# Four attention and feed-forward layers on one core: when the queue of SyncE issues the context, shared-weight and row loads of the first and fourth attention

## The reference

```
x = x + L0_attention(layernorm(x), ctx)   # 16 heads of 16, masked
x = x + L0_ffn(layernorm(x))              # 8 experts, top 1, and a shared part
x = x + L1_attention(layernorm(x), ctx)   # one head of 256
x = x + L1_ffn(layernorm(x))              # 8 experts, top 2, and a shared part
x = x + L2_attention(layernorm(x), ctx)   # 16 heads of 64
x = x + L2_ffn(layernorm(x))              # 8 experts, top 2
x = x + L3_attention(layernorm(x), ctx)   # 16 heads of 16, masked
x = x + L3_ffn(layernorm(x))              # one dense part, then a last layer norm
```

## Time and profile before

| what | value |
|---|---|
| median of 3 runs | 2320.24 us (2318.2 to 2321.33) |
| profiled execution, its own time | 2323.39 us |
| its span, first to last instruction | 2321.6 us |
| TensorE busy (matmul) | 2169.4 us, 93% |
| VectorE, ScalarE, GpSimd busy | 1285.7, 1074.0, 448.3 us |
| mean granted TensorE clock | 0.969 of full speed |
| DMA, share of 16 engines from 100 to 200 us | 0.72, at 182 GB/s |
| DMA, share of 16 engines from 2000 to 2100 us | 0.73, at 184 GB/s |

### The profile page before, as it was taken

One profiled execution on the slowest core, in us unless ns is written; L12 is line 12 of the kernel. 1 busy time (PEld: TensorE's weight loads), 2 busy tenths in 40 slices (PEclk: granted clock), 3 DMA queues, 4 the chain that ended last, 5 costly groups with the idle time before them and its releaser, 6 DMA issues.

```text
span 2321.6 us, 46633 instructions
## 1 busy us (share of the span) xinstructions
PE 2169.4 (93%) x16038; PEld 1759.9 (76%) x16038; DVE 1285.7 (55%) x3563; ACT 1074.0 (46%) x2929; POOL 448.3 (19%) x478
## 2 busy tenths in 40 slices
PE   7999989999988899999999999999959979988998
PEld 6888877777666667678888788888747758877888
DVE  6877873222244522556556556555542238778766
ACT  5878872222223122244444444444402237877863
POOL 3112201111153345100000000000014421121150
PEclk9999999999999799999999999999969989999999
DMA  8677746222265322110000000001232257767701
GB/s 211 184 193 181 183 116 276 79 86 91 71 178 166 128 66 68 41 46 8 19 27 16 12 14 13 12 8 48 95 113 62 64 143 185 188 175 178 179 19 33
DMA packets 154867, 230.65 MB, mean 99 GB/s; under 512 B 66608, under 2 KB 127488, under 8 KB 152336
## 3 DMA queue, kind: packets, MB, share of 16 engines
q1 hardware_dynamic: 142160, 196.07, 30.4%
q0 software_dynamic: 10656, 29.37, 4.1%
q10 hardware_dynamic: 1824, 2.23, 0.4%
HBM read 176.36 MB, written 51.25 MB: 98 GB/s over the span
## 4 chain that ended last, share of the span: by engine, by line
PE 77%; DVE 7%; DMA 5%; issue 4%; SPq 3%; ACT 2%; POOL 1%; ACTq 0%; DVEq 0%; POOLq 0%
PE bank L2012 9%; PE bank L1157 8%; PE bank L2045 6%; PE bank L1188 6%; PE bank L1043 6%; PE bank L1039 6%; PE bank L2077 5%; PE bank L1083 4%; PE bank L1142 4%; PE bank L1028 3%; PE bank L1135 3%; PE bank L2062 3%; SPq L1523 2%; DMA query_halves<-arena 2%; PE bank L2398 2%
## 5 line engine op out<-in xcount | busy, mean ns | idle before, releaser
L1157 PE MATMUL bank<-ident,arena 112*125 112x112 f32 x2352 | 376.0, 278 | 2.2 <-DVE arena L1395 0.3
L1157 PEld LDWEIGHTS bank<-ident,arena 112*125 112x125 f32 x2352 | 342.8, 191 | 32.2 <-ACT arena L1428 5.8
L1428 ACT ACTIVATE arena<-arena,mx 112x375 f32<-112x375 f32 x512 | 309.3, 605 | 108.6 <-DVE mx L1374 104.5
L1374 DVE CUSTOM_DVE_ANT_0 arena<-bank,maskf 112x375 f32<-112x375 f32 x512 | 272.8, 541 | 101.3 <-PE bank L1135 96.8
L1428 ACT ACTIVATE arena<-bank,mx 112x375 f32<-112x375 f32 x272 | 154.8, 573 | 183.0 <-DVE mx L1386 155.4
L2012 PE MATMUL bank<-arena 128*128 x532 | 231.7, 558 | 2.1 <-ACT arena L2138 2.1
L1135 PE MATMUL bank<-kS,qS 128*112 128x376 f32 x512 | 204.9, 401 | 28.6 <-DMA qS<-query_halves 13.9
L1395 DVE COPY arena<-bank 125x336 f32<-125x336 f32 x448 | 214.1, 501 | 17.3 <-PE bank L1157 17.3
L1188 PE MATMUL bank<-arena 125*32 125x112 f32 (+1 forms) x4608 | 202.6, 265 | 3.1 <-DVE arena L1395 2.9
L1188 PEld LDWEIGHTS bank<-arena 125*32 125x32 f32 (+1 forms) x4608 | 144.3, 118 | 49.8 <-issue 32.5
L1435 ACT ACTIVATE arena<-bank 125x336 f32<-125x336 f32 x336 | 148.3, 442 | 45.4 <-PE bank L1157 44.4
(11 more groups left out here) (266 smaller groups left out, 3699.2 us busy)
## 6 DMA issues: line engine op xcount, KB each, us to landing
kS<-key_halves SPq DMA_DIRECT2D x256, 188.0 KB, 3.9
key_halves<-arena SPq DMA_DIRECT2D x64, 376.0 KB, 4.9
arena<-in_ctxT SPq DMA_DIRECT2D x62, 376.0 KB, 4.9
arena<-in_f_out SPq DMA_DIRECT2D x21, 768.0 KB, 4.5
qS<-query_halves SPq DMA_DIRECT2D x252, 56.0 KB, 2.2
arena<-in_f_up SPq DMA_DIRECT2D x4, 2816.0 KB, 20.0
arena<-results SPq DMA_DIRECT2D x38, 224.0 KB, 5.6
query_halves<-arena SPq DMA_DIRECT2D x32, 224.0 KB, 5.3
```

The source lines that it names most:

```text
L1157: m = pe.transpose(bank[2 + g % 2][0:KT, k * S:(k + 1) * S], pr[:, g % t.NR, k * KT:(k + 1) * KT], ident[0:S, 0:S])
L1374: dve.tensor_tensor_reduce(sm[:, g % 2, :], bank[g % 2][0:S, 0:SK], maskf[:, :], -t.a["scale"], 3e38, ALU.add, ALU.min, mx[:, g % t.NR:g % ...
L1428: act.activation(pr[:, g % t.NR, :], src, ACT.Exp, bias=mx[:, g % t.NR:g % t.NR + 1], scale=-1.0, accum_out=row_sum(t, b)[:, h:h + 1]).the ...
```

## The change

The loads that followed `batch(b)` become a function `loads(b)`. For b = 0, 1 and 2 it is called where the loads stood. `loads(3)` to `loads(14)` are called inside the next group, behind its spill of the queries and its spill of the first keys and ahead of its stackings. Nothing else moves; `loads(15)`, which would issue nothing, is not called.

```
                 spill_queries()
                 spill_keys(0)
+                if b > LOADS_LATE:
+                    loads(b - 1)
                 if b >= 2:
                     sp.wait_ge(t.scores, t.h0 + (b - 1) * t.H)
                 stack_queries()
...
-            for b in range(B):
-                batch(b)
+            LOADS_LATE = 3
+
+            def loads(b):
                 if t.L == 0 and b + 2 < B // 2:
                     rows_of_x(sp, b + 2)
...
+            for b in range(B):
+                batch(b)
+                if b < LOADS_LATE:
+                    loads(b)
```

## The result

| | before | after |
|---|---|---|
| median | 2320.78 us (2318.2 to 2325.83, 4 runs) | 2304.88 us (2301.49 to 2305.7, 4 runs) |
| ratio | | 0.9918 [0.9901, 0.9934] |
| profiled execution, own time (span) | 2323.39 (2321.6) us | 2305.7 (2303.8) us |

The kernel is 15.9 us faster by the medians, 17.7 by the profiled executions, 19 by the ratio. The forecast was 2306 us, with 2300 to 2320 as its range.

A forecast was written before the change was run, and what follows sets the result against it. TensorE, busy 93% of the span, was held by waits on stacked keys, which SP's queue ends. 12.8 us idle time plus 5.1 clock less 2.0 remnants gave 15.9 us: 2307.5 by profile, 2304.3 by median; 2306 taken, range 2300 to 2320.

The forecast's parts named there:

- Query spill earlier: SP's queue, group 5 of A0: the query spill is issued at 104.5 instead of 105.89, 1.4 us earlier.
- Query spill lands sooner: Group 5 of A0: without loads just ahead, the query spill lands in 4.0 us instead of 6.2.
- Loads between: SP's queue, group 5: loads issue while the query spill lands, so the query stacking goes at 108.8, 3.4 us earlier.
- The chain that comes late next: First key spill to last stacked key: 12.1 us, or 13.3 with a stretched query stacking, against 13.1 available.
- The idle time: TensorE's seven waits on stacked keys go: 5.6 us in A0 and 7.2 in A3, 12.8 us.
- The clock: TensorE's lowered clock behind the two longest waits goes with them: 5.1 us gained.
- remnants: Waits on stacked keys left over the 24 windows: 2.0 us put back, with bounds 0 and 12.8.
- The context at nothing: GpSimd's context load, issued 2.9 us later in group 5, costs 0; the leanest even context keeps 0.8 us spare.
- Partial: Rival, 0.20: three waits with nothing to spare (3.23, 1.44, 2.68 us) stay at half and the clock falls; 2310 to 2316.
- The bytes: Rival, 0.14: 872 KB of loads between spill and stacking make keys land as late as before; 2318 to 2322.
- The stacking as the bound: Rival, 0.11: at odd windows' first scores the chain takes 14.4 us, 1.3 over the 13.1; 2324 to 2332.
- It doesn't do what it says: Rival: if waits in groups 0 to 3 and at A3's start grew, nothing would help; counted with the bytes rival.

The follow-up runs named there:

- e2_fourth: The changed kernel with the loads moved in the fourth attention (A3) only, the first (A0) in the old order; 2313.61 us, 0.9946 of the kernel before.
- e3_between: The changed kernel with the moved loads between the query spill and the first key spill; 2302.8 us, 0.9916 of the kernel before.
- after_again: The changed kernel itself, unaltered, timed once more; 2300.4 us, 0.9915 of the kernel before.
- e6_context_stays: The changed kernel with the context load (376 KB) back ahead of the spills, the other loads still moved; 2311.89 us, 0.9947 of the kernel before.
- e4_behind_stackings: The changed kernel with all moved loads one step later, behind the stacking of the first keys; 2389.53 us (2 runs), 1.0292 of the kernel before.

## Why the prediction was right

**Query spill earlier: right in kind.** The key stacking of group 4 ends at 102.75 and the spill goes at 103.34, after 0.6 us of waiting for its evacuation; the issue of the three loads (1.4 us) is off its path.

**Query spill lands sooner: right, undersized.** Assumed 4.0 us, measured 3.3 against the 6.2 of the earlier trace rows. I had put this down to the loads ahead alone; by the rows of e2_fourth it also takes a queue that hardly pauses before the spill. Over groups 5 to 12 of A0 the spills landed in 4.8 to 6.4 us before and in 2.3 to 4.8 us after.

**Loads between: right.** The stacking follows the last load without a pause (107.66, 107.76). The cover was shorter than assumed, since the spill lands 1.1 us before it; e3_between takes most of that 1.1 us away (3.2 us from spill to stacking, 2.9 for the landing), without a gain in time.

**The chain that comes late next: mis-sized here.** I worked out 12.1 us from key spill to the last stacked key, 13.3 with the long stacking, against 13.1 to be had. From 105.74 to 119.38 are 13.6 us, with TensorE ready at 118.87, 13.1 us after the spill. The key stacking was stretched (2.74 against 1.86 us). But this is the one window with moved loads in which it shows, and in after_again there is none.

**The idle time: low. The clock: right.** Forecast 12.8 less 2.0 of remnants, 10.8 us; measured 13.2 in the two stages. The remnants were 0.5 us, and line 1354 took 1.1 us less, with 1.2 us less of waits at line 1083 behind it, which the sum did not have. Clock: forecast 5.1, and the stretches at 0.50 that are gone are worth 5.1. The sum has no term for the other 1.6 us by which the busy time fell. TensorE at the changed place, answering to the earlier trace rows:

```profile
122.00:124.00 2.00, 2.00 (x34) 1.72 (x34) 1.97 (x8) 1.38 (x6) 0.00 (x0) 1.00 1.03 238
124.00:126.00 2.00, 2.00 (x16) 2.00 (x15) 1.53 (x6) 1.93 (x5) 0.00 (x0) 1.00 0.85 179
```

So the stages gave 19.9 us against a sum of 15.9. Of these, 17.8 us are left in the spans. The medians give 15.9, but the ratio's interval is 15 to 23 us, and after_again gave 21.6: the agreement to a microsecond is chance.

**The context at nothing: right, for a reason only half seen.** Its wait grew from 78.3 to 99.1 us and the root kept a spare of 0.50 us, less than the 0.8 forecast. What I had missed is the other side: an early halving holds up VectorE, by 6.8 us in the two stages of e6_context_stays. And e4_behind_stackings shows the cliff that lies beyond the spare. The Trainium skill, DMA: Bandwidth & Descriptors, "Rules for kernel authors", says to issue a DMA early and wait late. Taken by itself that would have kept the context in front; measured, this costs about 7 us here.

**The rivals.** *Partial* fell: the three waits without a margin are 0.51 us, nothing and nothing. *The bytes* fell: the engines moved 193 and 191 GB/s in the stages instead of 185 and 182 and the keys came in time. *The stacking as the bound* had its first sign (13.6 against 13.1 us) in one window of twelve, not in all. *It doesn't do what it says* fell: the order on SP is as described, and the wait at the start of A3 stayed, at 10.7 us.

## What to carry to other kernels

In a strictly ordered DMA queue, a write that is read back at once should not stand directly behind loads that are needed a window later; put the loads where the queue would wait for the write's landing anyway. Then measure how much spare the moved load had left, at its leanest place, because the loss beyond it (85 us) is several times the gain (16 to 20). And compare stretches of equal work, idle and busy apart: that shows the clock and the small collisions that are easily missed in the list of waits. An instruction that at times takes several times its usual length, as lines 1354 and 849 do, points at such a collision.

## What the runs showed of the hardware that was not expected

- VectorE's line 1354 took 0.35 us alone and up to 1.97 us beside GpSimd's halving (a 128x752 cast, then a tensor_tensor); it ended 0.14 to 0.16 us after one of them. Line 849, also a tensor_scalar from SBUF to SBUF, did the same (up to 1.81 us). Line 1374, which reads PSUM, kept its mean (542 ns in e6_context_stays and in the changed kernel).
- 47 DMAs of 64 bytes, each of 16 pieces of 4 bytes from DRAM to DRAM, made the kernel about 46 us slower than the changed one. The same number with one element, and 26 with the 16 pieces going into SBUF, cost nothing that could be measured.
- The clock in the first 60 us, where the kernels don't differ, was 0.94 in the profiled executions of the kernel before and of the changed kernel, and 1.00 in after_again, with 2.0 us less of busy time than in the changed kernel. Such a difference belongs to no edit:

```profile
0.00:60.00 60.00, 48.94 (x379) 40.66 (x380) 39.72 (x127) 34.09 (x98) 20.26 (x35) 0.94 0.84 210
```

and the same stretch of after_again:

```profile
0.00:60.00 60.00, 46.90 (x390) 37.87 (x391) 41.62 (x131) 34.91 (x102) 20.31 (x35) 1.00 0.83 210
```
